# GpSimd's additions in four instructions and its pair sums in two, with a new order on all engines

## What is computed

```python
x = x + _L0_conv_ref(_gn(x), ...)
x = x + _L1_conv_ref(_gn(x), w1, w2, w3)

# _gn: G = 32 groups for 32 channels: each channel of an image is normalised over its 64 x 64 pixels
# _L0_conv_ref
v = jnp.einsum('bchw,dc->bdhw', x, value_w)
patches = ...                                   # the 3x3 neighbours of v, zero padded
mu = jax.nn.softmax(gate, axis=1)               # R = 4 gates a pixel, from x
kern = jnp.exp(-(pu / sig_u) ** 2 - (ps / sig_s) ** 2)   # from theta, base, hyper of x
w = mu * kern
w = w / (jnp.sum(w, axis=(1, 2), keepdims=True) + 1e-06)
agg = jnp.einsum('brsl,bcsl->brcl', w, patches).reshape(Bb, R * C, Hh, Ww)
return jnp.einsum('bkhw,ok->bohw', agg, pw_w) + pw_b[None, :, None, None]
# _L1_conv_ref: three 3x3 convolutions, 32 -> 64 -> 64 -> 32 channels
```

## Time and profile before

| | us |
|---|---|
| median of 3 runs | 541.21 (540.34 to 541.48) |
| the profiled execution | 541.46 |
| its span, first to last instruction | 539.6 |
| TensorE busy | 470.1 (87%) |
| VectorE busy | 419.2 (78%) |
| ScalarE busy | 207.2 (38%) |
| GpSimd busy | 199.9 (37%) |

### The profile page before, as it was taken

How to read it: one execution, slowest core, us unless ns; L and a number is a source line. 1 busy time by engine, 2 the same in 40 slices (tenths; PEclk the granted TensorE clock), 3 DMA queues, 4 the chain that set the end, 5 groups by cost and what they waited for, 6 DMA issues and landing times.

```text
span 539.6 us, 6937 instructions
## 1 busy us (share of the span) xinstructions
PE 470.1 (87%) x2498; PEld 386.1 (72%) x2498; DVE 419.2 (78%) x553; ACT 207.2 (38%) x386; POOL 199.9 (37%) x95
## 2 busy tenths in 40 slices
PE   1249563899898999899999999999979999999995
PEld 1238353766786788678886897878767878787894
DVE  2799998889998998978898989898988989221211
ACT  3522412374156434372428314751537324341110
POOL 2164347801682175208470359027540613000000
PEclk9999795699999999999999999999999999999999
DMA  5100002600117100731072014501361035108201
GB/s 151 39 4 1 0 27 54 145 19 1 40 36 172 38 28 17 160 73 47 4 162 67 13 40 110 112 22 40 76 137 33 0 79 130 33 1 183 57 0 39
DMA packets 38225, 32.21 MB, mean 60 GB/s; under 512 B 24112, under 2 KB 28720, under 8 KB 38192
## 3 DMA queue, kind: packets, MB, share of 16 engines
q1 hardware_dynamic: 38192, 31.77, 24.7%
HBM read 5.66 MB, written 4.19 MB: 18 GB/s over the span
## 4 chain that ended last, share of the span: by engine, by line
PE 55%; DVE 22%; ACT 7%; issue 7%; POOL 3%; SPq 3%; DMA 2%; DVEq 0%; ACTq 0%; POOLq 0%
PE conv_ps L407 41%; DVE prod L1116 9%; PE val_ps L458 4%; PE agg_ps L473 4%; SPq L277 2%; DVE prod L1126 2%; PE conv_ps L421 2%; PE pw_ps L488 2%; POOL gn L1888 2%; PE geo_ps L440 2%; DMA xq<-y 2%; ACT L1542 1%; ACT c_lo L1595 1%; DVE y L1159 1%; DVE st L950 1%
## 5 line engine op out<-in xcount | busy, mean ns | idle before, releaser
L1116 DVE TENSOR_TENSOR prod<-val_ps,tapw 128x2048 f32<-128x2048 f32 x80 | 180.5, 2283 | 9.8 <-PE val_ps L458 8.5
L1902 POOL TENSOR_TENSOR prod<-prod 128x2048 f32<-128x2048 f32 x23 | 108.3, 4711 | 173.3 <-DVE prod L1116 173.3
L407 PE MATMUL conv_ps<-c_hi,wc_hi 128*128 128x448 f32 (+2 forms) x384 | 152.3, 397 | 1.1 <-ACT c_lo L1595 1.1
L407 PE MATMUL conv_ps<-c_hi,wc_lo 128*128 128x448 f32 (+2 forms) x384 | 144.3, 376 | 0.0
L407 PE MATMUL conv_ps<-c_lo,wc_hi 128*128 128x448 f32 (+2 forms) x384 | 144.2, 375 | 0.0
L407 PEld LDWEIGHTS conv_ps<-c_hi,wc_hi 128*128 128x128 f32 x384 | 72.6, 189 | 15.6 <-issue 5.0
L1918 POOL TENSOR_TENSOR xs<-xn 128x1024 f32<-128x1024 f32 x32 | 72.5, 2275 | 29.2 <-PE val_ps L458 17.0
L1126 DVE TENSOR_TENSOR prod<-prod 128x2048 f32<-128x2048 f32 x35 | 81.7, 2336 | 0.4 <-issue 0.2
L407 PEld LDWEIGHTS conv_ps<-c_hi,wc_lo 128*128 128x128 f32 x384 | 72.3, 188 | 10.4
L407 PEld LDWEIGHTS conv_ps<-c_lo,wc_hi 128*128 128x128 f32 x384 | 72.7, 189 | 8.1
L1587 ACT ACTIVATE c_hi<-conv_ps 128x512 fp32r<-128x512 f32 (+4 forms) x88 | 41.5, 484 | 87.5 <-PE conv_ps L407 87.0
(11 more groups left out here) (106 smaller groups left out, 440.6 us busy)
## 6 DMA issues: line engine op xcount, KB each, us to landing
xq<-y SPq DMA_DIRECT2D x128, 132.0 KB, 2.6
xraw<-in_x SPq DMA_DIRECT2D x32, 128.0 KB, 2.7
x2r<-x SPq DMA_DIRECT2D x128, 32.0 KB, 1.9
out_y<-x2r SPq DMA_DIRECT2D x32, 128.0 KB, 2.8
prod<-in_w SPq DMA_DIRECT2D x1, 576.0 KB, 5.2
xn<-xn SPq DMA_DIRECT2D x16, 24.8 KB, 1.8
prod<-in_w SPq DMA_DIRECT2D x1, 384.0 KB, 3.5
prod<-in_w SPq DMA_DIRECT2D x1, 192.0 KB, 2.5
```

What stands on the lines that cost most here:

```text
L407: mm = nc.tensor.matmul(bank[:, 0:conv_cols(n)], weights, lo if part == 1 else hi, start=term == part == 0, stop=final and part == 2)
L1116: v.tensor_tensor(dst, val.unsqueeze(2).to_broadcast([P, B, R, C]), wgt.unsqueeze(3).to_broadcast([P, B, R, C]), ALU.mult).then_inc(mult_d ...
L1902: p.tensor_tensor(product(i, TAPS * h + a), product(i, TAPS * h + a), product(i, TAPS * h + b), ALU.add).then_inc(add_g, 1)
```

## The change

In GpSimd's add_products one instruction on 2048 columns becomes four on 512, and in pair_sum one on 16 rows becomes two on 8. The semaphore is raised by the last. The semaphores' counts, who adds what, and the work of all engines are the same. The order lists of TensorE, VectorE, ScalarE and GpSimd are changed in many places, mostly by one to three steps; SP's isn't.

```diff
+PIECES, PROD = 4, 2048
...
-                p.tensor_tensor(product(i, TAPS * h + a), product(i, TAPS * h + a), product(i, TAPS * h + b),
-                                ALU.add).then_inc(add_g, 1)
+                for q in range(PIECES):
+                    at = slice(q * PROD // PIECES, (q + 1) * PROD // PIECES)
+                    op = p.tensor_tensor(product(i, TAPS * h + a)[:, at], product(i, TAPS * h + a)[:, at],
+                                         product(i, TAPS * h + b)[:, at], ALU.add)
+                op.then_inc(add_g, 1)
...
-                p.tensor_tensor(xs[:, n], xn[:, a[0], a[1]], xn[:, b[0], b[1]], ALU.add).then_inc(pairs_done, 1)
+                for q in range(2):
+                    r0, r1 = q * QR // 2, (q + 1) * QR // 2
+                    top, bottom = (slice(t[0].start + r0, t[0].start + r1) for t in (a, b))
+                    op = p.tensor_tensor(xs[:, n, r0:r1], xn[:, top, a[1]], xn[:, bottom, b[1]], ALU.add)
+                op.then_inc(pairs_done, 1)
```

The order on TensorE in the front (image 0 and the start of the convolutions):

```diff
             geometry(0)
+            values(0, 0)
             gn1_sums(1, 0)
-            values(0, 0)
             values(0, 1)
             gn1_sums(1, 1)
             values(0, 2)
             fold(0, 0)
-            fold(0, 1)
             values(0, 3)
+            geometry(1)
             values(0, 4)
-            geometry(1)
             values(0, 5)
+            values(0, 6)
             transpose_sums(0, 0)
-            values(0, 6)
             transpose_sums(0, 1)
             values(0, 7)
             transpose_sums(0, 2)
+            values(0, 8)
+            fold(0, 1)
             transpose_sums(0, 3)
-            values(0, 8)
...
             gn2_sums(0, 0)
-            values(1, 6)
             gn1_sums(2, 0)
             gn2_sums(0, 1)
             gn1_sums(2, 1)
+            values(1, 6)
             values(1, 7)
-            transpose_sums(1, 0)
             geometry(2)
-            transpose_sums(1, 1)
             values(1, 8)
             values(1, 9)
+            transpose_sums(1, 0)
+            convs(0, 0, 3)
+            transpose_sums(1, 1)
+            convs(0, 3, 5)
+            values(2, 0)
+            convs(0, 5, 6)
             transpose_sums(1, 2)
+            convs(0, 6, 8)
             transpose_sums(1, 3)
-            convs(0, 0, 8)
             take_high(0, 0)
```

TensorE at the end of layer 0 of the last image:

```diff
             transpose_sums(7, 7)
-            convs(6, 27, 29)
+            convs(6, 27, 30)
+            take_high(6, 5)
+            convs(6, 30, 32)
             pointwise(7, 1)
-            convs(6, 29, 34)
-            take_high(6, 5)
-            convs(6, 34, 36)
+            convs(6, 32, 37)
             take_high(6, 6)
-            convs(6, 36, 38)
             gn2_sums(7, 0)
-            convs(6, 38, 40)
+            convs(6, 37, 40)
             take_high(6, 7)
```

VectorE, front and last image:

```diff
             mult(0, 0)
+            mult(0, 1)
             gn1_bias(1)
-            mult(0, 1)
             mult(0, 2)
...
             gn2_scale(6)
+            add_products(7, 0, 2)
             gn2_bias(6)
             mult(7, 5)
             split_low(6)
-            add_products(7, 0, 2)
+            add_products(7, 0, 3)
+            mult(7, 6)
+            mult(7, 7)
             result(5, 0)
-            mult(7, 6)
-            add_products(7, 0, 3)
-            mult(7, 7)
             mult(7, 8)
+            add_products(7, 1, 1)
             result(5, 1)
-            add_products(7, 1, 1)
+            mult(7, 9)
             add_products(7, 1, 2)
-            mult(7, 9)
             add_products(7, 1, 3)
```

ScalarE, front:

```diff
             tap_weights(0, 5)
+            norm1(1)
             fold(0, 0)
-            norm1(1)
+            tap_weights(1, 0)
             norm1_padded(1)
-            tap_weights(1, 0)
             sums_out(0, 0)
             tap_weights(1, 1)
             sums_out(0, 1)
             tap_weights(1, 2)
-            fold(0, 1)
             sums_out(0, 2)
             tap_weights(1, 3)
+            tap_weights(1, 4)
             sums_out(0, 3)
-            tap_weights(1, 4)
+            fold(0, 1)
...
             norm1_padded(2)
+            norm1(2)
             norm2(0)
             split_high(0)
-            norm1(2)
```

More of the change, by code:

```diff
@@ L569, in _ @@
             take_high(0, 0)
[L570 removed]
             take_high(0, 1)
+            convs(0, 8, 14)
+            pointwise(1, 0)
+            convs(0, 14, 15)
             take_high(0, 2)
[L573 to L582 removed]
+            convs(0, 15, 17)
@@ L604, in _ @@
             gn1_sums(3, 1)
             take_high(0, 7)
+            gn2_sums(1, 0)
+            values(2, 6)
+            convs(0, 40, 42)
             gn2_sums(1, 1)
-            convs(0, 39, 42)
+            convs(0, 42, 44)
+            values(2, 7)
+            convs(0, 44, 47)
+            take_high(0, 8)
             transpose_sums(2, 0)
-            convs(0, 42, 45)
-            values(2, 7)
-            convs(0, 45, 48)
+            convs(0, 47, 49)
             values(2, 8)
-            convs(0, 48, 49)
@@ L664, in _ @@
+            convs(1, 45, 46)
             gn1_sums(4, 0)
-            take_high(1, 7)
+            take_high(1, 8)
             gn2_sums(2, 1)
+            gn1_sums(4, 1)
+            convs(1, 46, 54)
             values(3, 9)
-            gn1_sums(4, 1)
-            take_high(1, 8)
-            convs(1, 45, 53)
+            geometry(4)
+            convs(1, 54, 58)
             transpose_sums(3, 0)
-            convs(1, 53, 54)
-            geometry(4)
+            convs(1, 58, 59)
+            values(4, 0)
@@ L674, in _ @@
+            convs(1, 59, 60)
             transpose_sums(3, 1)
-            convs(1, 54, 60)
+            convs(2, 0, 1)
             transpose_sums(3, 2)
-            convs(2, 0, 3)
-            values(4, 0)
+            convs(2, 1, 3)
+            transpose_sums(3, 3)
+            values(4, 1)
+            convs(2, 3, 4)
             take_high(2, 0)
-            convs(2, 3, 7)
-            transpose_sums(3, 3)
-            convs(2, 7, 10)
+            pointwise(3, 0)
+            convs(2, 4, 11)
@@ L863, in _ @@
+            values(7, 0)
+            convs(5, 15, 16)
+            pointwise(6, 0)
+            convs(5, 16, 18)
+            take_high(5, 3)
+            transpose_sums(6, 4)
+            convs(5, 18, 20)
+            transpose_sums(6, 5)
             values(7, 1)
-            take_high(5, 2)
-            convs(5, 16, 17)
-            take_high(5, 3)
-            convs(5, 17, 23)
+            convs(5, 20, 23)
+            transpose_sums(6, 6)
+            convs(5, 23, 27)
             take_high(5, 4)
-            convs(5, 23, 24)
@@ L881, in _ @@
[L881 to L884 removed]
+            take_high(5, 7)
             values(7, 4)
[L886 to L887 removed]
+            convs(5, 37, 38)
+            values(7, 5)
             pointwise(6, 1)
[L889 to L895 removed]
@@ L896, in _ @@
-            gn2_sums(6, 1)
-            convs(5, 44, 54)
+            convs(5, 38, 44)
+            gn2_sums(6, 0)
+            convs(5, 44, 45)
+            gn2_sums(6, 1)
+            convs(5, 45, 47)
+            take_high(5, 8)
+            values(7, 6)
+            convs(5, 47, 57)
+            transpose_sums(7, 0)
             values(7, 7)
-            convs(5, 54, 60)
+            convs(5, 57, 58)
+            transpose_sums(7, 1)
+            convs(5, 58, 59)
             values(7, 8)
-            convs(6, 0, 3)
@@ L1290, in _ @@
             mult(3, 5)
+            residual(2, 1)
             mult(3, 6)
-            residual(2, 1)
+            add_products(3, 0, 2)
             mult(3, 7)
```

609 lines of the change are left out of this document (290 added, 319 removed).

## The result

| | before | after |
|---|---|---|
| median, us | 541.35 (540.34 to 541.49) | 544.56 (543.95 to 545.53) |
| ratio | | 1.0065 (95%: 1.0050 to 1.0079) |
| span of the profiled execution, us | 539.6 | 542.1 |
| TensorE's mean granted clock | 0.97 | 0.96 |

The account below looks back on a forecast made before the run. VectorE was taken to set the pace up to 106 us, TensorE from 165 us, both nearly full between. Gains of 2.5 us up to 165 us and 0.9 at split_low(2) sum to 3.4, giving 537.8 us, range 531.5 to 543.5.

Parts of the forecast that it names:

- Line 1043 and the front: VectorE's addition near 53 us waits about 1.1 us for a piece instead of 4.32; VectorE about 3.3 us earlier at 105.
- the 2.3 forecast for 62 us: VectorE at 62 us, front of the kernel: reckoned 2.5 us earlier, taken as 2.3.
- The price of a piece: GpSimd: each further instruction taken at 0.05 us, so +0.15 us per addition, +0.05 per pair sum, 205 us busy.
- Rival C: GpSimd's additions: a further instruction costs near 0.55 us, making the kernel slower, about 545 us (542.3 to 547); chance 0.20.
- slack of 0.7 us per image: At add_products(i,0,2): GpSimd's addition ends at 141.97 us, VectorE starts at 142.67; +1.65 us per addition would cost 0.95 per image.
- TensorE would start convs(0) about 2.5 us sooner: Start of image 0's convolutions: 2.5 us sooner, three groups of transpose_sums(1) still to do; TensorE's own gain about 0.5 us.
- The rest can only fill TensorE's 3.81 us of idle time; I take 2.0: 106 to 165 us: the rest of VectorE's 3.3 us gain fills TensorE's idle time, worth 2.0; sum to 165 us -2.5.
- The rest of the order's moves I put at nothing; TensorE's queue covers them: After 165 us: other moves cost nothing under TensorE's 97% full queue; 3.5 us lost if each image waits 0.5.
- split_low(2): VectorE step after 165 us feeding DMAs: halved pair sums cut its 1.61 us wait to about 1.0; 0.9 us gained.
- my rivals: Whole kernel: further gain to 533.5 us (chance 0.16), nothing at 541 (0.22), slower at about 545 (0.20).

Follow-up runs that it names:

- e18: Kernel before, old order, with pair sums in two instructions and only image 0's additions in four: 537.9 us, ratio 0.9934.
- e1: Kernel before, every order list as before, with all GpSimd pieces (additions in four, pair sums in two): 540.0 us, ratio 0.9985.
- e15: Changed kernel with unused matmuls and transposes filling TensorE's idle time between 76 and 103 us only: 543.6 us, ratio 1.0037.
- e5: Kernel before with all pieces and the new order only up to about 88 us (front): 541.6 us, ratio 0.9998.
- e6: Kernel before with all pieces and the new order only from about 88 to 141 us (middle): 541.4 us, ratio 0.9994.
- e7: Kernel before with all pieces and the new order only behind about 141 us (late part): 540.8 us, ratio 0.9983.
- e12: Kernel before with all pieces and the new order up to about 141 us (front and middle), old behind it: 544.8 us, ratio 1.0081.
- e17: Kernel before, old order, with only the pair sums in two instructions, additions whole: 539.5 us, ratio 0.9965.
- e16: Kernel before, old order, with only the additions in four instructions, pair sums whole: 542.9 us, ratio 1.0028.
- e13: Changed kernel with unused TensorE work as fillers only behind 76 us, including 8 matmuls ahead of gn1_sums(3,0): 543.5 us, ratio 1.0025.
- e3: Changed kernel with 14 unused matmuls added on TensorE behind values(1,6): 544.8 us, ratio 1.0068.
- e2: Changed kernel with its new order kept but GpSimd's additions and pair sums whole again: 549.3 us, ratio 1.0153.
- e9: Kernel before, old order, with all pieces and unused TensorE work filling its idle time in the front: 539.0 us, ratio 0.9967.
- e10: Changed kernel with unused TensorE work as fillers from 16 us on, including 8 matmuls ahead of gn1_sums(3,0): 543.1 us, ratio 1.0043.
- e4: Changed kernel with 14 unused matmuls behind values(1,6) and 8 more ahead of gn1_sums(3,0): 544.1 us, ratio 1.0054.

## Why the prediction was wrong

- **Line 1043 and the front: right.** mult(0,4) at 42.5 us, line 1043 near 1.1 (measured 1.36), mult(0,7) at about 55 (54.66). VectorE passes at the border of two pieces. residual(0,0) came 1.4 us earlier, less than the 2.3 forecast for 62 us.
- **The price of a piece: too low.** 0.05 us was taken, 0.14 measured. An addition takes 0.43 us more instead of 0.15, GpSimd is at 218.8 us instead of 205. The Trainium skill ("GPSIMD Engine Reference", section "2.1 Instruction dispatch") puts the dispatcher's call at tens of cycles for each instruction, which I had set at the same 0.05 us; the trace has 0.14 us for all that a further instruction adds, more than that estimate, and doesn't show how much of it is the call. Rival C, which names this mechanism, was to decide from 0.25 us, and its slack of 0.7 us per image was never used up by 0.43. Yet e18 against e1 shows the 21 additions of the later images to cost 2.1 us: they cost below the point where I had let them.
- **"TensorE would start convs(0) about 2.5 us sooner": 1.5.** TensorE now stands idle for 1.07 us ahead of it, which it didn't before. The sixteen DMAs behind split_low(0) begin only 0.35 us earlier (96.93 instead of 97.28 us). That it now waits for these transfers is argued from those times; the view names no releaser.
- **"The rest can only fill TensorE's 3.81 us of idle time; I take 2.0": this step failed.** The idle time did shrink a little, to 59 - 55.64 = 3.36 us. But I had counted the busy time as fixed. With convs(0) moved ahead of three groups of transposes and gaps in front of it, TensorE did 5.2 + 6.8 us of its work at half the rate. With the clock up in the same order (e15) 3.75 us of the loss before convs(1) are gone. The row that should have warned me stood in my own view: the clock column, 0.86 in the first stage and 1.00 in the second, and it leaves out the part before about 48 us. I never asked at which instruction it changes over, and what keeps it from changing later.
- **"The rest of the order's moves I put at nothing; TensorE's queue covers them": this step failed too.** Each part alone is nearly free (e5, e6, e7), front and middle together cost 0.96% (e12 to e1). The cover, a queue full to 97%, was reckoned at TensorE's upper level, and the moves themselves took that level away.
- **split_low(2): the mechanism was right.** It fell from 2.83 to 1.67 us. The gain belongs to the pair sums (e17): from convs(1) to convs(2) it is 0.9 us, just what was taken. Another 0.6 us come between convs(3) and convs(4), which I had counted at nothing; in all e17 gains 1.8 us.
- Slower by a changed clock was none of my rivals. The three that I had argued on waits and on the price of an instruction. C's 545 us is near the measured 544.6 by luck: its condition, 0.25 us or more for a further piece, wasn't met.

## What to carry to other kernels

Where the engine that sets the pace has two clock levels, find the instruction at which its clock rises, and price every reordering ahead of that point and every new idle microsecond behind it in the lower level's durations. Time parts of a change apart: here a gain of 0.35%, one of 0.31%, a loss of 0.51% and one of 0.80% stood in one diff, and the best kernel measured takes the first two only. Where a kernel's executions differ, one profile is one of them: compare its time with the others before reading a total from it. Split an instruction that holds up its neighbour only where that neighbour is seen waiting for it.

## What the hardware showed that I had not expected

- TensorE fell to the lower level behind idle times of 2.01 us (after, at 141.6), 1.92 (e16, at 223.2), 2.20 (e13, at 224.6), 1.95 (e3, at 148.3) and 1.47 (e6, at 138.3), and stayed there for 3.4 to 6.8 us though it was busy throughout. It didn't fall behind 1.86 us at 223.1 in the kernel before, behind 1.95 and 2.19 us in e15, nor behind 2.43 us in e2 (at 230.5). So the length of the idle time alone doesn't separate the cases. The same wait in e3, with a fall to 0.56 behind it, and in e15, without:

```profile
150.24 1.11 PE L460 MATMUL val_ps<-ident_sb,xs 128*128 128x128 f32 x4 [1.95 <-DVE prod L1126]
```
```profile
149.10 0.66 PE L460 MATMUL val_ps<-ident_sb,xs 128*128 128x128 f32 x4 [1.95 <-DVE prod L1134]
```

- Fillers between 16 and 34 us (e9, e10) didn't hold the clock up: it was 0.61 and 0.57 from 26 to 34 us with 6.57 and 5.64 us of 8 busy.
- Two executions of one and the same sequence of instructions may be 2.5 us apart at 104 us (e3 and e4), by the durations of TensorE's transposes around 50 us.
